# The mean of squares behind the gated output, summed in two single passes, with the rest of the squares formed on GpSimd

## What is computed

```python
q = _l2norm(_short_conv(hidden_states @ Wq, conv_q)) * SCALE     # H=16 heads of 128
k = _l2norm(_short_conv(hidden_states @ Wk, conv_k))
v = _short_conv(hidden_states @ Wv, conv_v)
...
def step(S, inp):                                   # over time
    S = S * jnp.exp(gt)[..., None]
    err = jnp.einsum('bhk,bhkv->bhv', kt, S)
    delta = bt[..., None] * (vt - err)
    S = S + kt[..., None] * delta[:, :, None, :]
    return (S, jnp.einsum('bhk,bhkv->bhv', qt, S))
...
gate = (hidden_states @ Wg + bg).reshape(B, T, H, DV)
y = o * jax.nn.silu(gate)
y = y * jax.lax.rsqrt(jnp.mean(y * y, -1, keepdims=True) + EPS) * norm_w
return y.reshape(B, T, H * DV) @ Wo
```

## Time and profile before

| what | value |
|---|---|
| device time, median of 3 runs | 6108.75 us (6107.04 to 6117.89) |
| the profiled execution | 6114.65 us, its span 6112.9 us |
| PE busy, share of the span | 5887.2 us, 96% |
| DVE busy | 4404.6 us, 72% |
| ACT busy | 3050.3 us, 50% |
| POOL busy | 1806.4 us, 30% |

### The profile page before, as it was taken

The page is one execution under the profiler, slowest core; times in us unless marked ns, Lnnn a source line. Parts: engine busy times, 40 slices in busy tenths (PEclk is TensorE's granted clock), DMA queues, the critical chain, the costliest instruction groups (busy, mean ns, idle before and its releaser), DMA issues. The chain is left out here.

```text
span 6112.9 us, 92718 instructions
## 1 busy us (share of the span) xinstructions
PE 5887.2 (96%) x33208; PEld 4267.3 (70%) x33208; DVE 4404.6 (72%) x7563; ACT 3050.3 (50%) x5133; POOL 1806.4 (30%) x1636
## 2 busy tenths in 40 slices
PE   5699999999999999999999999999999999899999
PEld 2477777777777777777777777777777777544444
DVE  7788888888888888888888888888888888311110
ACT  2455555555555555555555555555555555301101
POOL 2233333333333333333333333333333333100000
PEclk8899999999999999999999999999999999899999
DMA  2101111111011111111011111110101111231221
GB/s 83 38 22 35 29 35 29 35 28 34 26 32 29 35 28 31 33 28 34 26 33 28 35 28 35 28 35 27 31 27 35 29 28 28 69 106 62 80 78 47
DMA packets 183711, 236.04 MB, mean 39 GB/s; under 512 B 25048, under 2 KB 128088, under 8 KB 179168
## 3 DMA queue, kind: packets, MB, share of 16 engines
q1 hardware_dynamic: 111072, 188.22, 10.3%
q10 hardware_dynamic: 72192, 41.95, 2.2%
HBM read 183.75 MB, written 46.38 MB: 38 GB/s over the span
## 5 line engine op out<-in xcount | busy, mean ns | idle before, releaser
L632 PE MATMUL bank<-xT,weights 128*128 128x512 f32 x4096 | 2160.1, 615 | 29.6 <-PEq L153 29.6
L1264 POOL TENSOR_TENSOR KR<-KR,decay_u 128x256 f32<-128x256 f32 x896 | 910.4, 1016 | 3048.9 <-PE bank L658 3048.9
L896 DVE SCALAR_TENSOR_TENSOR conv<-pre,taps,conv 128x512 f32<-128x512 f32 x1152 | 1082.0, 948 | 18.0 <-ACT conv L1104 8.9
L911 DVE TENSOR_TENSOR KQ<-KQ,decay_u 128x512 f32<-128x512 f32 x896 | 695.3, 776 | 497.1 <-PE bank L658 496.7
L658 PEld LDWEIGHTS bank<-KQ,KR 128*128 128x128 f32 x7168 | 905.8, 191 | 188.5 <-issue 181.4
L658 PE MATMUL bank<-KQ,KR 128*128 128x128 f32 x7168 | 962.5, 277 | 4.3 <-DVE KQ L911 3.2
L931 DVE COPY_PREDICATED all_pairs<-level_mask,bank 128x512 f32<-128x512 int32 x896 | 795.0, 887 | 0.0
L632 PEld LDWEIGHTS bank<-xT,weights 128*128 128x128 f32 x4096 | 663.3, 192 | 184.0 <-issue 161.2
L1149 ACT ACTIVATE T_inv<-bank 128x256 fp32r<-128x256 f32 x640 | 250.0, 391 | 956.7 <-PE bank L700 956.7
L681 PEld LDWEIGHTS bank<-T_inv,pairs 128*128 128x128 f32 x3072 | 464.9, 192 | 366.8 <-issue 333.1
L681 PE MATMUL bank<-T_inv,pairs 128*128 128x64 f32 x3072 | 713.9, 358 | 0.7 <-DVE T_inv L947 0.5
(11 more groups left out here) (160 smaller groups left out, 8701.9 us busy)
## 6 DMA issues: line engine op xcount, KB each, us to landing
decay_u<-decay_scratch SPq DMA_DIRECT2D x128, 510.0 KB
beta_u<-beta_scratch SPq DMA_DIRECT2D x128, 256.0 KB
y_scratch<-y_rn ACTq DMA_DIRECT2D x128, 256.0 KB, 2.3
y_in<-y_scratch SPq DMA_DIRECT2D x32, 1024.0 KB, 4.8
xt<-in_L_attn_hidden_states SPq DMA_DIRECT2D x8, 1024.0 KB, 5.2
x_in<-in_L_attn_hidden_states SPq DMA_DIRECT2D x32, 256.0 KB, 5.0
out<-o_out ACTq DMA_DIRECT2D x32, 256.0 KB, 2.0
w<-in_L_ffn_W SPq DMA_DIRECT2D x8, 704.0 KB, 5.0
```

The source lines that it names most:

```text
L632: last = nc.tensor.matmul(bank[w % 2][:], weights[par][:, w, k, :], xT[:, k, u % J * UC:(u % J + 1) * UC], start=k == 0, stop=k == KC - 1)
L896: nc.vector.scalar_tensor_tensor(conv[:, w], pre[:, w, :, t:t + P], taps[par][:, w, t:t + 1], conv[:, w], ALU.mult, ALU.add).then_inc(step ...
L911: nc.vector.tensor_tensor(second_halves, second_halves, pair[:, :, 0:1].unsqueeze(1).to_broadcast([P, 2, blocks, 1 << l]), ALU.mult).then_ ...
L1264: nc.gpsimd.tensor_tensor(first_halves, first_halves, second.to_broadcast([P, UC >> (l + 1), 1 << l]), ALU.mult).then_inc(keys_scaled.sem, 1)
```

## The change

The sum of the output's squares is now made as the sums for keys and queries are. ACT writes `y_sq` rounded to F32R. GpSimd computes the exact square of `yg` into `rnorm[:, 0]`, a buffer of the key and query norms that is free at that time, and then `y_sq_rest`, the exact square less the rounded one, in F32R. PE multiplies both with the matrix of ones in single passes that add up in `bank[2]`. The division by 128 moves into the scale of ACT's logarithm, and `mean_ones` goes. PE waits for the rest in place of the square; ACT waits for the rest before it writes `rnorm[:, 0]`.

On GpSimd the new function waits for yg, for the sums of the unit before (which read `y_sq_rest`) and for the last reading of `rnorm[:, 0]`, and between its two passes for the first of them and for y_sq. It stands after the key scaling of level 3.

```diff
-    mean_ones = sb("mean_ones", [P, P])
...
-    y_sq = sb("y_sq", [P, UC])
+    y_sq = sb("y_sq", [P, UC], F32R)
+    y_sq_rest = sb("y_sq_rest", [P, UC], F32R)
...
-                wait(pe, y_sq_ready, c, 1)
-                nc.tensor.matmul(bank[2][:], mean_ones[:], y_sq[:], start=True, stop=True).then_inc(y_sums_done.sem, 1)
+                wait(pe, y_rest_ready, c, 1)
+                nc.tensor.matmul(bank[2][:], ones_r[:], y_sq[:], start=True, stop=False)
+                nc.tensor.matmul(bank[2][:], ones_r[:], y_sq_rest[:], start=False, stop=True).then_inc(y_sums_done.sem, 1)
...
+                if w == 0 and c is not None:
+                    wait(act, y_rest_ready, c, 1)
                 nc.scalar.activation(rnorm[:, w], bank[2][:], ACT.Ln, bias=l2_eps[:, 0:1]).then_inc(sums_taken.sem, 1)
...
-                nc.scalar.activation(y_rn[:], bank[2][:], ACT.Ln, bias=ln_eps[:, 0:1]).then_inc(y_sums_free, 1)
+                nc.scalar.activation(y_rn[:], bank[2][:], ACT.Ln, bias=ln_eps[:, 0:1], scale=1.0 / P).then_inc(y_sums_free, 1)
...
+        def y_squares_left(u, hats_of):
+
+            if u is None:
+                return
+            wait_apart(pool, yg_ready.sem, yg_ready.at(u, 1), pool_waits_passed)
+            if u >= 1:
+                wait_apart(pool, y_sums_done.sem, y_sums_done.at(u - 1, 1), pool_waits_passed)
+            if hats_of is not None:
+                wait_apart(pool, hats_ready.sem, hats_ready.at(hats_of, 1), pool_waits_passed)
+            nc.gpsimd.tensor_tensor(rnorm[:, 0], yg[:], yg[:], ALU.mult).then_inc(y_square_ready.sem, 1)
+            wait_apart(pool, y_square_ready.sem, y_square_ready.at(u, 1), pool_waits_passed)
+            wait_apart(pool, y_sq_ready.sem, y_sq_ready.at(u, 1), pool_waits_passed)
+            nc.gpsimd.tensor_tensor(y_sq_rest[:], rnorm[:, 0], y_sq[:], ALU.subtract).then_inc(y_rest_ready.sem, 1)
...
                 scale_keys(s.m, 1 - s.odd, l)
+                if l == 3:
+                    y_squares_left(s.c, s.m)
```

More of the change, by code:

```diff
@@ L252, in _ @@
             nc.gpsimd.memset(ones[:], 1.0)
-            nc.gpsimd.memset(mean_ones[:], 1.0 / P)
             nc.gpsimd.memset(ln_eps[:], LN_EPS)
@@ L516, in attention @@
     y_sq_ready = signal("y_sq_ready", 1)
+    y_square_ready = signal("y_square_ready", 1)
+    y_rest_ready = signal("y_rest_ready", 1)
     square_ready = signal("square_ready", 2)
```

## The result

| | before | changed |
|---|---|---|
| device time, median | 6108.66 us (6107.04 to 6117.89, 4 runs) | 6580.37 us (6566.49 to 6599.24, 4 runs) |
| ratio | | 1.0771, 95% interval 1.0742 to 1.0800 |
| span of the profiled execution | 6112.9 us | 6580.0 us |
| granted clock over the span | 0.987 | 0.938 |

The change costs 472 us. I had forecast 170. The sign, the place and the length of PE's new wait were right. What was missed is larger than all that I had summed: behind the longer wait PE runs at half its clock, and that alone is some 300 us.

A forecast was written before the change was run, and what follows sets the result against it. PE's fixed order and its wait for DVE's ZI were taken to bound the kernel. ZI's delay of +207 less PE's gain of 37 gave +170 us, 6279 us as a median; range 6215 to 6325.

The forecast's parts named there:

- What bounds the kernel: PE's fixed order sets the unit's length; its one weighty wait is L700 for DVE's ZI, some 0.65 us a unit.
- GpSimd's passes against DVE: After level 3's key scaling, the new passes hold DVE's convolution steps and halo copy; ZI comes 1.76 us later, +207 in all.
- The copy's term: Halo copy before ZI waits for GpSimd's squares' product; ZI's delay is 1.76 us with it, 1.35 without (that rival: 0.12).
- the extra 0.08 us: Behind L700, if the squares' rest goes ahead of DVE's scaling L911, at most 0.08 us more a unit.
- PE's gain: Output squares' sums on PE: two single passes replace one full-precision pass, gaining 0.29 us a unit, 37 us.
- The slack at T_inv: At L681's weight load, which waits for DVE's T_inv: about 0.24 to 0.29 us of slack for PE's gain.
- the last rival: More than counted: held steps behind ZI, or PE's 2.4 us idle lowers the clock; 0.3 to 0.5 us a unit, chance 0.07.

The follow-up runs named there:

- passes set apart: Changed kernel with GpSimd's product moved ahead of the key scaling of level 3 and its rest ahead of that of level 5: 6069.05 us.
- when it was moved: Changed kernel with the halo copy on DVE put ahead of the four state updates instead of behind them: 6635.08 us.
- PE's part alone: Changed kernel with PE's two single passes but no rest formed by GpSimd; the second pass reads a tile of zeros: 6066.37 us.
- two quarters moved: Changed kernel with two quarters of the query projection moved on PE from behind L701 to in front of it: 6169.78 us.
- memset: Kernel before, with one memset of 448 columns on DVE in front of the ZI of level 5: 6181.14 us.
- product held: Changed kernel with GpSimd's product where it stands and only the rest moved ahead of the key scaling of level 5: 6255.55 and 6245.5 us.
- one quarter moved: Changed kernel with one quarter of the query projection (0.86 us) moved on PE in front of L701: 6333.24 and 6337.77 us.
- reduction of 820: Kernel before, with a reduction of 820 columns on DVE in front of the ZI of level 5: 6408.45 us.
- reduction of 1640: Kernel before, with one reduction of 1640 columns on DVE in front of the ZI of level 5: 6618.79 us.

## Why the prediction was wrong

- **What bounds the kernel**: right. PE's order and its wait for ZI set the unit's length. (The 0.65 us are the mean of 23 waits; not every unit has one.)
- **GpSimd's passes against DVE**: right to within 0.05 us at each step. The steps of 1.20 and 1.64 us, the copy of about 0.6, the wait of 2.4 us are in the trace, and their total on L701 is +206.5 us for +207. By kind of unit the wait is 2.41 us in an ordinary one (0.66 before) and 1.94 where the halo is a memset (0.59 before), +1.35 as forecast; where a memset stands for the state updates it is 1.45, and the unit itself, where the clock held, is 1.0 us longer than with the passes set apart (39.78 for 38.77), as forecast. The copy's term, which rested on one case at the loop's start, held in 93 of the trace's 112 copies, at 0.56 or 0.57 us, and a second time when it was moved. What remained open, which of L1280 and L913 goes first, came out for L913 in all 92 cases of a start that close, so the extra 0.08 us isn't there.
- **PE's gain**: 0.29 us a unit was mis-sized; it is 0.37 by the ordinary unit (39.37 to 39.00 us). That would be 47 us for 128 units, and the two profiled executions are 47.7 us apart; the medians differ by 40.6 us, and why they don't show all of it is open. The slack at T_inv did suffice.
- **The clock**: this is the step that failed. It stood as the last rival, "the longer idle of PE lowers the clock", at a chance of 0.07 and a price of 0.3 to 0.5 us a unit. The price was 2.35 us a unit: 6580 less the 6279 of the sum, over 128. The wait's length was in my own sum, 2.4 us in a row, nearly four times what the rows showed at full clock. I took the clock of 1.00 at 0.66 us as reason to expect 1.00 at 2.4 us, where it gave no price either way. A rival of unknown price should have been bounded: the kernel before shows the lower level too (a clock of 0.73 from 100 to 220 us, where PE is busy for 59 of 120 us), and the 3.6 us of work behind L701, at half speed, would cost as much again.
- **The range**: it ended at 6325, below that rival's own upper end of 6345, and no end was set by a unit at half the clock.

By the runs, the 472 us are: -41 for the single passes, +207 for ZI's delay, and about +306 for the clock, the remainder. The remainder agrees with PE's busy time: 6147.3 us, against 5839.9 with PE's part alone, is 307 us more for the same work. The Trainium skill's rule on the shared SBUF interfaces (GPSIMD Engine Reference, section 1 Specifications) agrees with these traces in its half on two SBUF inputs: such convolution steps took 1.20 and 1.64 us. The copy, which has one SBUF input and took 0.49 and 0.57 us, would come under its half on 2-port modes; no run here shows in which mode it ran.

## What to carry to other kernels

An engine's idle time says when its queue is free, not whom its work will hold up: before a pass goes to GpSimd, list what DVE does in the same microseconds, and put the pass beside DVE's waits and its PSUM work. Two passes in other places turned +7.7% into -0.6%. And a new wait on the matrix engine has two prices, its own length and the clock behind it; when a sum puts a longer wait in a row on PE than any row at full clock shows, price the lower clock too, or give PE work to do meanwhile.

## What the runs showed of the hardware

- A wait of PE costs more than itself as it grows. Waits made in different ways, with the clock over 1000 to 4000 us, the time, and the units of the loop (those that begin between 330 and 4900 us) in which the clock falls:

| kernel | mean of PE's waits for ZI, us | clock | units with the lower clock | time, us |
|---|---|---|---|---|
| before | 0.65 | 1.00 | 0 of 116 | 6109 |
| passes apart | 0.66 | 1.00 | 0 of 117 | 6069 |
| two quarters moved | 0.63 | 0.98 | 43 of 115 | 6170 |
| memset | 1.01 | 1.00 | 7 of 115 | 6181 |
| product held | 1.13 | 0.98 | 50 of 113 | 6251 |
| one quarter moved | 1.38 | 0.97 | 59 of 112 | 6336 |
| reduction of 820 | 1.50 | 0.97 | 73 of 110 | 6408 |
| changed kernel | 2.24 | 0.94 | 97 of 106 | 6580 |
| reduction of 1640 | 2.36 | 0.95 | 86 of 105 | 6619 |

  The wait alone doesn't order them: two quarters moved has the shortest wait and a clock of 0.98. What else of PE's work counts is open.
- The lower clock starts near the end of the wait or after it, and reaches into the work behind. In the changed kernel it starts between 0.4 us before L701 and 1.9 us after it; in the unit shown it is 0.50 in most of the six to seven us that follow the wait.
- GpSimd and DVE take turns by whole instructions where both read SBUF and DVE's instruction has two SBUF inputs or is the small copy: the one that comes second waits for the first one's end, for copies of 24 columns (0.49 and 0.57 us instead of 0.17) as for steps of 512 (1.20 and 1.64 instead of 0.75). Who is second goes by the order of issue, but not to the last 0.01 us: where DVE's L913 starts 0.01 us after GpSimd's L1280, L913 goes first, 92 times of 92. State updates with one input in PSUM pass unhindered, 1.11 us for four beside a product and a scaling.
